# One Trainium2 core, gated cross-attention with experts: the weighted sums of a slot moved behind the next slot's first pair of scores

## The chip, the cores and the metric

The kernel runs on one core of one Trainium2 chip. The metric is the device time of one execution in microseconds (us); the median of the runs stands for a kernel. The engines are named as in the profile: PE (TensorE, matmul), PEld (its weight loads), DVE (VectorE), ACT (ScalarE), POOL (GpSimd), SP (SyncE, which issues DMAs).

## What is computed

Cut to what matters here:

```python
def layer(x, ctx):                       # x (16, 512, 256), ctx (16, 1601, 128), all f32
    n = layernorm(x)
    y = attention(n Wq, n Wk, n Wv, causal)          # 16 heads of 16
    y = y + attention(n Wcq, ctx Wck, ctx Wcv)       # 16 heads, 1601 keys
    x = x + tanh(g_xattn) * (y Wp + bp)
    n = layernorm(x)
    return x + tanh(g_ffn) * (top4_of_32_experts(n) + shared_expert(n))
```

For each head the softmax runs over the 512 causal keys of the text, and a second one over the 1601 keys of the context; the two weighted sums of values are added.

## The kernel before

**Three stages.** A short prologue (part "P") prepares batch 0. Then 16 parts follow, one for each batch ("F", 14 times "M", "L"), which do the attention. They also finish the batch before (output projection, second layer norm, router, shared expert, scatter to the experts' slots) and prepare the next one. A last part "X", the experts and a merge come after them. The change lies in the 16 parts alone.

**Slots.** A part is 68 slots. A slot is one tile of 128 keys against 512 queries for 4 heads: `slot_of(n)` gives for each group g of 4 heads (4 groups) 13 tiles of context keys ("cross", the last with 65 keys) and then 4 tiles of text keys ("self"). A self tile `kt` takes only the queries from 128*kt on. Counted through a part, the self slots are 13 to 16, 30 to 33, 47 to 50 and 64 to 67.

**What a slot holds.** PE writes scores transposed, keys on partitions, in pairs of heads: `scores(part, n, 0)` and `scores(part, n, 1)`, two matmuls each (L442), into a ring of three PSUM buffers, so that score i waits until exponential i-3 is done (L440). ACT takes the exponential of each (L627) into `prob`, which has two halves by the parity of the slot; it waits for the weighted sums of two slots ago. In self slots POOL zeroes the masked triangle of all four heads in one instruction (L966), after the fourth exponential, in `mask`, which stands in POOL's second half of the slot. PE then forms the weighted sums (`weighted`, L464): four f32 matmuls in four groups of 32 columns, shown as eight instructions, into one PSUM bank `outs` in which a softmax's 13 or 4 slots accumulate. For a cross slot `weighted(part, n)` waits until the fourth exponential of slot n is done, for a self slot until its mask is. At the first tile of a softmax it also waits for `copied`: ACT has copied the sums of the softmax before out of the bank (`outs`, L637), which stands at the end of ACT's slot, behind the four exponentials.

**Items.** The softmax's maxima are computed apart and a group ahead: PE writes tiles of scores with queries on partitions (L520, L527, L536 and L537) to a ring of four PSUM banks (`ring`), and DVE reduces each with a maximum (L780). These tiles and all the projections of the neighbouring batches are "items". `plan(kind)` writes the order out: it deals fixed items to half slots and fills the rest with maxima so that a load in estimated us is level. Each of the 136 half slots of a part has a list, `items[2 * n + pair]`, that every engine walks in the same order. What the change calls the maxima of a slot is such a list. Of the 52 cross slots of an "M" part, 23 have a list for their second half with at most two maxima of 512 columns and no projection in it. One of them is slot 39, where the router's softmax stands: `soft_a` on ACT waits for DVE. In slot 16 POOL comes to `inverse_root` (16 small instructions, L953 to L959, for the second layer norm), which waits for DVE's statistics and stands ahead of that slot's mask.

**The order on PE.** Engines take their instructions in the program's order. PE's order in a part is `run` of `pe_program`. ACT's is `exps`, items, `exps`, items, `outs` of the slot before; POOL's has the mask in the second half. The change touches `run` of `pe_program` alone.

Of the kernel before, what the change touches and what calls it, by code (L numbers as in the profile page):

```python
# [106 lines left out]
def slot_of(n):  # L107

    ch, r = divmod(n, SLOTS // 2)
    v, r = divmod(r, NCT + NQ)  # L110
    return (ch, v, "cross", r) if r < NCT else (ch, v, "self", r - NCT)


def shape_of(kind, kt):

    if kind == "cross":
        return (128 if kt < NCT - 1 else REST), 0, kt, T + 128 * kt
    return 128, 128 * kt, NCT + kt, 128 * kt
# [19 lines left out]
def value_items(ch):  # L138
    return [("value", ch, 4 * i, min(4, NCT - 4 * i)) for i in range(4)] + [("value", ch, NCT, NQ)]
# [92 lines left out]
def build_attention(nc, B, x, ctx_t, w, scr, stacks, wall):  # L232
# [6 lines left out]
    with ExitStack() as ctx:  # L239
# [151 lines left out]
        def read(eng, part, it, i=0, **how):  # L391

            p = PLANS[part.kind]
            eng.wait_ge(freed[p.bank[it, i]], part, p.turn[it, i], **how)
# [27 lines left out]
        def pe_program(eng):  # L422
# [8 lines left out]
            def scores(part, n, pair):  # L431
                ch, v, kind, kt = slot_of(n)
                m, q0, _, k0 = shape_of(kind, kt)
                qc = 0 if kind == "cross" else T
                g = 2 * ch + v
                for p in range(2):
                    j, i = 2 * pair + p, 4 * n + 2 * pair + p
                    k = i % SB
                    before = i - SB if i >= SB else max(j for j in range(4 * SLOTS) if j % SB == k) - 4 * SLOTS
                    pe.wait_ge(exped, part, before + 1)  # L440
                    pe.wait_ge(rowed[g], part, row_no(g))
                    eng.matmul(ps[0:m, k, q0:T], kst[g][0:KR + 2, j, k0:k0 + m],  # L442
                               qst[g][0:KR + 2, j, qc + q0:qc + T], start=True, stop=True).then_inc(scored.sem, 1)

            def weighted(part, n):

                ch, v, kind, kt = slot_of(n % SLOTS)
                m, q0, vi, _ = shape_of(kind, kt)
                last = kt == (NCT if kind == "cross" else NQ) - 1
                if kind == "cross":  # L450
                    pe.wait_ge(exped, part, 4 * n + 4)
                else:
                    pe.wait_ge(masked, part, 4 * (2 * ch + v) + kt + 1 - (16 if n < 0 else 0))
                if kt == 0:
                    pe.wait_ge(copied, part, 4 * ch + 2 * v + (kind == "self"))
                if n == 0:
                    for k in range(RB):
                        pe.wait_ge(freed[k], part, 0)
                if n == SLOTS // 2:
                    for it in value_items(1):  # L460
                        read(pe, part, it)
                for j in range(4):
                    hl = 4 * v + j
                    mm = eng.matmul(po[32 * j:32 * j + 32, q0:T], vt[ch][0:m, VW * vi + VE * hl:VW * vi + VE * hl + 32],  # L464
                                    prob[0:m, n % 2, j, q0:T], start=kt == 0, stop=last)
                    if j == 3:
                        mm.then_inc(summed.sem, 1)
# [120 lines left out]
            def run(part):  # L588
                items = PLANS[part.kind].items
                if part.kind in "PX":  # L590
                    for here in items:
                        for it in here:
                            item(part, it)
                    return
                for n in range(SLOTS):
                    for pair in range(2):
                        scores(part, n, pair)
                        for it in items[2 * n + pair]:
                            item(part, it)
                    if n or not part.first:  # L600
                        weighted(part, n - 1)

            start = Part("P", 0, B - 2)
            pe.wait_ge(loaded, start, LOADS)
            pe.wait_ge(consts, start, CONSTS)
            pe.wait_ge(setup, start, 3)
            run(start)
            run(Part("F", 0, B - 2))
            for b in range(1, B - 1):
                run(Part("M", b, B - 2))  # L610
# [1071 lines left out]
```

## Time and profile before

| what | us |
|---|---|
| median of 3 runs | 4988.99 (4988.46 to 4994.27) |
| profiled execution, its own time | 5012.8 |
| its span in the trace | 5011.0 |
| PE busy in the span | 4348.2 (87%) |
| DVE busy | 3558.0 (71%) |
| ACT busy | 2689.2 (54%) |
| POOL busy | 1685.3 (34%) |
| granted clock of PE, mean over the span | 0.957 |

The profiled execution took 5012.8 us, of which 1.8 lie outside the span; it is 0.5% longer than the median. Busy is the time in which an engine has an instruction at work. Matmuls are pipelined, and a row of two matmuls of 512 columns shows 0.60 us although the next matmul starts 0.44 after the first of them. So distances between starts are read here, not lengths, where the pace of PE matters.

### The profile page before, as it was taken

The page shows a single profiled execution, that of the slowest core. Times are in us where ns is not written, and L with a number is a line of the kernel's source. Part 1 is how long each engine was busy: PE and PEld are TensorE (multiplying, and loading weights), DVE is VectorE, ACT ScalarE, POOL GpSimd, SP SyncE. Part 2 cuts the span into 40 slices and gives each one's busy share as a digit, 9 for nine tenths or more (in the row PEclk, how much of TensorE's full clock was granted, in tenths as well). Part 3 has the DMA queues.
Part 4 walks back from the last instruction along what each step waited for, and adds up shares of the span by engine and source line. Part 5 has one row for each costly group of instructions (what it writes and reads, how often), then busy time and mean ns, then how long its engine had stood idle before and what let it go on. Part 6 is the DMA issues. An engine that isn't in the chain of part 4 may idle for free. (4 is left out here: it accounts for less than half of the span.)

```text
span 5011.0 us, 75640 instructions
## 1 busy us (share of the span) xinstructions
PE 4348.2 (87%) x25312; PEld 1888.4 (38%) x25312; DVE 3558.0 (71%) x7731; ACT 2689.2 (54%) x5523; POOL 1685.3 (34%) x2170
## 2 busy tenths in 40 slices
PE   4899999999999999999999999999999961777872
PEld 1333333333333333333333333334343411566662
DVE  4788878877778777878787878787878732344443
ACT  0565656565656565656565656565656550444441
POOL 3122323232323232323232323232323131577773
PEclk7999999999999999999999999999999985899996
DMA  4444545453544443445454544444544436788888
GB/s 91 81 89 78 108 78 108 79 107 80 102 84 102 82 104 82 105 78 109 77 108 77 109 77 108 78 108 78 105 81 101 69 95 153 130 137 134 136 138 251
DMA packets 363510, 513.36 MB, mean 102 GB/s; under 512 B 64052, under 2 KB 227766, under 8 KB 363190
## 3 DMA queue, kind: packets, MB, share of 16 engines
q1 hardware_dynamic: 252022, 372.60, 35.9%
q0 software_dynamic: 88064, 115.69, 13.3%
q10 hardware_dynamic: 23104, 20.97, 1.4%
q8 instruction: 181, 2.97, 0.3%
q14 instruction: 139, 1.14, 0.1%
HBM read 288.77 MB, written 201.29 MB: 98 GB/s over the span
## 5 line engine op out<-in xcount | busy, mean ns | idle before, releaser
L627 ACT ACTIVATE prob<-scores 128x512 f32<-128x512 f32 (+3 forms) x4352 | 2151.5, 560 | 1333.9 <-PE scores L442 1308.6
L780 DVE TENSOR_REDUCE pmx<-ring 128x1 f32<-128x512 f32 (+1 forms) x3328 | 2000.4, 662 | 188.9 <-PE ring L520 172.0
L442 PE MATMUL scores<-stacks 98*128 98x512 bf16 (+3 forms) x4352 | 1270.7, 369 | 71.1 <-ACT prob L627 36.5
L464 PE MATMUL outs<-prob,vt 128*32 128x512 f32 x8704 | 1099.9, 578 | 11.0 <-POOL prob L966 10.0
L520 PE MATMUL ring<-stacks 96*128 96x512 bf16 x3072 | 985.8, 389 | 90.5 <-DVE pmx L780 79.7
L442 PEld LDWEIGHTS scores<-stacks 98*128 98x128 bf16 (+1 forms) x4352 | 337.7, 99 | 1247.0 <-ACT prob L627 716.4
L1523 POOL DMA_INDIRECT scratch_sums<-e_yo,e_tok x320 | 497.9, 1556 | 230.8 <-DVE e_yo L1486 130.5
L780 DVE TENSOR_REDUCE mc<-ring 128x1 f32<-128x128 f32 (+3 forms) x1024 | 437.4, 482 | 151.2 <-PE ring L537 113.7
L966 POOL TENSOR_SCALAR_AFFINE_SELECT prob<-prob 128x512 f32<-128x512 f32 x256 | 168.5, 658 | 1075.0 <-ACT prob L627 1073.3
L520 PEld LDWEIGHTS ring<-stacks 96*128 96x128 bf16 x3072 | 303.0, 99 | 516.4 <-DVE pmx L780 244.4
L1035 POOL TENSOR_TENSOR split<-rest,split 128x512 bf16<-128x512 f32 (+1 forms) x224 | 218.8, 977 | 819.0 <-DVE split L858 818.5
L1345 PE MATMUL e_ph<-e_xt,e_we 128*128 128x256 f32 x1280 | 322.2, 395 | 129.8 <-ACT e_xt L1381 126.7
L855 DVE SCALAR_TENSOR_TENSOR rest<-ring,bcol,split 128x512 f32<-128x512 f32 (+1 forms) x224 | 153.1, 684 | 270.8 <-ACT split L661 268.8
L536 PE MATMUL ring<-stacks 96*128 96x128 bf16 (+3 forms) x1024 | 272.3, 309 | 55.9 <-DVE mc L780 20.1
L1345 PEld LDWEIGHTS e_ph<-e_xt,e_we 128*128 128x128 f32 x1280 | 232.1, 191 | 214.7 <-ACT e_xt L1381 171.5
L464 PEld LDWEIGHTS outs<-prob,vt 128*32 128x32 f32 x8704 | 172.4, 109 | 354.1 <-issue 316.0
L1486 DVE TENSOR_SCALAR e_yo<-e_py,e_wcol 128x256 f32<-128x256 f32 x320 | 140.1, 479 | 213.5 <-DMA scratch_sums<-e_yo,e_tok 195.3
L1024 POOL DMA_INDIRECT scratch_slots<-split,rows x256 | 253.4, 990 | 106.5 <-issue 69.8
L1390 ACT COPY e_we<-stacks 128x768 f32 x160 | 133.6, 835 | 155.5 <-issue 140.3
L661 ACT ACTIVATE split<-ring,bcol 128x512 bf16<-128x512 f32 (+1 forms) x224 | 142.2, 637 | 137.2 <-PE ring L491 107.9
L537 PE MATMUL ring<-maskb,identb 128*128 128x128 bf16 x1024 | 211.7, 223 | 0.0
L1466 DVE SCALAR_TENSOR_TENSOR e_sl<-e_th,e_ph 128x256 f32<-128x256 f32 x160 | 67.4, 421 | 189.9 <-ACT e_th L1400 189.9
(155 smaller groups left out, 3891.9 us busy)
## 6 DMA issues: line engine op xcount, KB each, us to landing
stacks<-scratch_parts SPq DMA_DIRECT2D x768, 128.0 KB, 7.1
stacks<-scratch_parts SPq DMA_DIRECT2D x384, 136.1 KB, 10.2
scratch_parts<-split SPq DMA_DIRECT2D x64, 768.0 KB, 4.4
e_xin<-scratch_slots SPq DMA_DIRECT2D x160, 289.0 KB
scratch_parts<-split SPq DMA_DIRECT2D x32, 816.8 KB, 4.5
num<-oc POOLq DMA_DIRECT2D x256, 64.0 KB
den<-scratch_inverses POOLq DMA_DIRECT2D x64, 256.0 KB, 9.0
ct<-in_ctx_t_dram SPq DMA_DIRECT2D x16, 800.5 KB, 8.1
```

The source lines that it names most:

```text
L442: eng.matmul(ps[0:m, k, q0:T], kst[g][0:KR + 2, j, k0:k0 + m], qst[g][0:KR + 2, j, qc + q0:qc + T], start=True, stop=True).then_inc(scored ...
L464: mm = eng.matmul(po[32 * j:32 * j + 32, q0:T], vt[ch][0:m, VW * vi + VE * hl:VW * vi + VE * hl + 32], prob[0:m, n % 2, j, q0:T], start=kt ...
L520: eng.matmul(dst, qst[g][0:KR, j, 128 * qt:128 * qt + 128], kst[g][0:KR, j, T + 512 * of:T + 512 * of + 512], start=True, stop=True).then_ ...
L536: eng.matmul(dst[:, 0:n], qst[g][0:KR, j, T + 128 * qt:T + n], kst[g][0:KR, j, 0:n], start=True, stop=False)
L537: eng.matmul(dst[:, 128 * qt:n], identb[:, :], maskb[:, :], start=False, stop=True).then_inc(ring.sem, 1)
L627: eng.activation(prob[0:m, n % 2, j, q0:T], ps[0:m, i % SB, q0:T], ACT.Exp, scale=SCALE).then_inc(exped.sem, 1)
L780: eng.tensor_reduce(dst, src, AX.X, ALU.max).then_inc(free_of(part, it), 1)
L966: eng.affine_select(out=prob[:, n % 2, :, q0:q0 + 128], in_=prob[:, n % 2, :, q0:q0 + 128], compare_op=ALU.is_ge, fill=0.0, base=0, patter ...
L1024: eng.indirect_dma_start(scr["slots"], bass.IndirectOffsetOnAxis(ap=rows[:, NQ * k + q:NQ * k + q + 1].bitcast(U32), axis=0), xs[:, ROW * ...
L1035: eng.tensor_tensor(last, rest[:, no % 2, 0:n], mid, ALU.subtract).then_inc(low.sem, 1)
L1345: op = eng.matmul(phd[i][:, m, :], we[u][:, c0:c0 + H], xt[i][:, kc, :], start=kc == 0, stop=kc == KC - 1)
L1523: eng.indirect_dma_start(scr[f"sums{i}"], bass.IndirectOffsetOnAxis(ap=tok[u][:, q:q + 1].bitcast(U32), axis=0), yo[i][:, q, :], None, com ...
```

## The change

In a slot n, PE's program had: scores of pair 0, first list of items, scores of pair 1, second list of items, weighted sums of slot n-1. With the change it has: scores of pair 0, weighted sums of slot n-1, first list, scores of pair 1, second list. No instruction is added or taken away; the other engines' programs and all waits' values are the same.

```diff
                 for n in range(SLOTS):
                     for pair in range(2):
                         scores(part, n, pair)
+                        if pair == 0 and (n or not part.first):
+                            weighted(part, n - 1)
                         for it in items[2 * n + pair]:
                             item(part, it)
-                    if n or not part.first:
-                        weighted(part, n - 1)
```

## Rows read from the trace of the kernel before

**Rows 1.** Page, busy time and slices: PE, DVE and PE's granted clock.

```profile
PE 4348.2 (87%) x25312; PEld 1888.4 (38%) x25312; DVE 3558.0 (71%) x7731; ACT 2689.2 (54%) x5523; POOL 1685.3 (34%) x2170
...
PE   4899999999999999999999999999999961777872
```

**Rows 2.** Busy time by stretch, a batch's worth: PE, PEld, DVE, ACT, POOL, clock, DMA, GB/s.

```profile
1770.00:2040.00 270.00, 251.57 (x1483) 94.22 (x1480) 216.35 (x469) 158.62 (x321) 75.90 (x116) 0.97 0.47 98
```

**Rows 3.** The scores' line: number, shortest/median/longest ns, first and last start.

```profile
L442 PE MATMUL scores<-stacks x4352: 217/379/634, 127.7 to 4102.5; 98*128 98x512 bf16 x151, 98*128 98x128 bf16 x12, 98*128 98x256 bf16 x12, 98*128 98x384 bf16 x12
```

**Rows 4.** Waits over the whole span: us in total, times, longest.

```profile
PE ring L520 <- DVE pmx L780: 79.7, 116, 5.4
...
PE scores L442 <- ACT prob L627: 36.5, 82, 1.2
```

**Rows 5.** Groups by line, engine PE: weighted sums and causal maxima, idle before them.

```profile
L464 PE MATMUL outs<-prob,vt 128*32 128x512 f32 x8704 | 1099.9, 578 | 11.0 <-POOL prob L966 10.0
...
L536 PE MATMUL ring<-stacks 96*128 96x128 bf16 (+3 forms) x1024 | 272.3, 309 | 55.9 <-DVE mc L780 20.1 <-DMA stacks<-scratch_parts 14.6 <-DVE rest L855 5.5
```

**Rows 6.** Timeline of PE, one light cross slot (slot 9 of a batch).

```profile
1900.32 0.60 PE L442 MATMUL scores<-stacks 98*128 98x512 bf16 x2
1900.75 0.60 PE L520 MATMUL ring<-stacks 96*128 96x512 bf16 x2
1901.28 1.06 PE L464 MATMUL outs<-prob,vt 128*32 128x512 f32 x8
1902.28 0.61 PE L442 MATMUL scores<-stacks 98*128 98x512 bf16 x2
```

**Rows 7.** Timeline of ACT in the same slot.

```profile
1899.65 2.18 ACT L627 ACTIVATE prob<-scores 128x512 f32<-128x512 f32 x4 [0.90 <-PE scores L442]
```

**Rows 8.** Timeline of DVE, slots 5 to 10 of that batch.

```profile
1887.58 18.05 DVE L780 TENSOR_REDUCE pmx<-ring 128x1 f32<-128x512 f32 x30 [0.87 <-PE ring L520]
```

**Rows 9.** Timeline of PE, the old sums in self slot 48.

```profile
2055.20 1.06 PE L464 MATMUL outs<-prob,vt 128*32 128x512 f32 x8
```

**Rows 10.** Timeline of POOL, the mask of slot 48.

```profile
2055.59 0.63 POOL L966 TENSOR_SCALAR_AFFINE_SELECT prob<-prob 128x512 f32<-128x512 f32 x1 [2.22 <-ACT prob L627]
```

**Rows 11.** Timeline of PE, slots 64 to 67 (end of the batch).

```profile
2112.33 1.06 PE L464 MATMUL outs<-prob,vt 65*32 65x512 f32 x8
...
2115.05 1.06 PE L464 MATMUL outs<-prob,vt 128*32 128x512 f32 x8
...
2120.03 0.59 PE L442 MATMUL scores<-stacks 98*128 98x512 bf16 x2 [0.51 <-DMA stacks<-mr]
```

**Rows 12.** Timeline of POOL, the masks of slots 64, 65 and 66.

```profile
2112.93 0.64 POOL L966 TENSOR_SCALAR_AFFINE_SELECT prob<-prob 128x512 f32<-128x512 f32 x1 [0.35 <-ACT prob L627]
2116.24 0.91 POOL L966 TENSOR_SCALAR_AFFINE_SELECT prob<-prob 128x512 f32<-128x512 f32 x1 [2.68 <-ACT prob L627]
2117.12 1.08 POOL L1035 TENSOR_TENSOR split<-rest,split 128x512 bf16<-128x512 f32 x1
2118.17 0.67 POOL L966 TENSOR_SCALAR_AFFINE_SELECT prob<-prob 128x512 f32<-128x512 f32 x1
```

**Rows 13.** Timeline of PE, slot 16 into 17.

```profile
1925.94 0.23 PE L536 MATMUL ring<-stacks 96*128 96x128 bf16 x1 [1.23 <-DVE mc L780]
...
1927.27 1.08 PE L464 MATMUL outs<-prob,vt 128*32 128x256 f32 x8
1928.28 1.03 PE L442 MATMUL scores<-stacks 98*128 98x512 bf16 x2
```

**Rows 14.** Timeline of POOL, the mask of slot 16, behind the Newton steps.

```profile
1930.14 0.64 POOL L966 TENSOR_SCALAR_AFFINE_SELECT prob<-prob 128x512 f32<-128x512 f32 x1
```

**Rows 15.** Timeline of PE, slots 39 and 41: where it waits for ACT and DVE.

```profile
2021.41 0.39 PE L442 MATMUL scores<-stacks 98*128 98x512 bf16 x1 [1.12 <-ACT prob L627]
...
2028.94 0.52 PE L520 MATMUL ring<-stacks 96*128 96x512 bf16 x1 [3.24 <-DVE pmx L780]
```

**Rows 16.** Busy time by stretch around slot 16 (columns as in the first such view).

```profile
1926.00:1930.00 4.00, 3.83 (x19) 1.19 (x20) 2.38 (x7) 1.07 (x2) 2.79 (x15) 0.58 0.00 0
```

## The prediction
> **What bounds the kernel now.** I read the page's slices first. PE is busy nine tenths or more in the 29 slices after the first two and before the fall at the end, 87% over the span [rows 1]. That is the stage of the 16 parts, the only one that the change touches. The 4352 score matmuls of that stage start between 127.7 and 4102.5 us [rows 3]: 3975 us for 1088 slots, 3.65 us a slot and 248 us a batch. In a stretch of 270 us PE is busy 251.6, DVE 216.4, ACT 158.6 and POOL 75.9 [rows 2]. So PE stands still for 18.4 us in 270, some 17 us a batch, and the rest is work in a fixed order. Then the waits: PE's largest kinds are small, 79.7 us for DVE to empty a bank and 36.5 us for ACT [rows 4], and in front of the 8704 rows of weighted sums it is idle for only 11.0 us in all [rows 5]. That last number is what the change puts at stake. The sums find their operands ready today because they come nearly a whole slot after the exponentials that they need.
>
> **What moves.** Nothing is added or removed. Seen along the queue, the end of a slot was: second list of items of slot n, weighted sums of n-1, first scores of n+1. It becomes: second list of n, first scores of n+1, weighted sums of n. Two things change: the scores come 1.0 us earlier against the items (the sums' pitch, 1901.28 to 1902.28 [rows 6]), and each set of sums comes one slot earlier. The pitches themselves I cost at nothing: each of score, sum and tile still has a neighbour of another kind, and only their order differs. No DMA is issued by PE, and no queue of POOL, SP, ACT or DVE has a step moved past another.
>
> **The new wait, and who is behind it.** The sums of n now wait for the fourth exponential of n (self slots: for the mask after it), with only the second list and one pair of scores as cover. Queued behind them on PE are the first list of n+1, which DVE needs, and the second pair of scores, which ACT needs. I price it by one subtraction: the time at which the operands are ready, less the time at which PE would come to the sums. The latter is today's start of the sums of n-1 plus the pitch of a pair of scores.
>
> *Light cross slots.* In slot 9 the old sums start at 1901.28, so the new place is 1901.28 + 0.44 = 1901.72 [rows 6]. The fourth exponential ends at 1899.65 + 2.18 = 1901.83 [rows 7], and about 0.06 us (my estimate, from the scale of the rows' distances) passes on the way: a wait of 0.16 us. With a third tile of 0.22 in the second list it is gone. The lists have 23 cross slots with at most two such tiles in the second half, one of them slot 39. Where ACT has another pass in front of the exponentials it is 0.3 to 0.5. I take 0.27 x 22 = 6.0 us a batch. At a softmax's first tile the copy of the bank comes on top; self slots hide it beside the mask, and the few others are within this figure.
>
> *Self slots.* In slot 48 the new place is 2055.20 + 0.22 (a pair of 256 columns, half of 0.44) = 2055.42, the mask ends at 2055.59 + 0.63 = 2056.22 [rows 9, 10]: 0.8 us. Of the eleven self slots before the last group, slot 16 left out, three have a projection or a long list behind them and cost nothing. For the other eight I let the pitch of the list and POOL's own work vary around this one, 0.1 to 1.3 us, and take 0.66 as their mean: 5.3 us a batch.
>
> *End of the batch.* Slot 64: place 2112.33 + 0.33 (the 0.44 for 384 columns), mask ready 2113.57: 0.9. Slot 65: place 2115.05 + 0.22, mask ready 2117.15: 1.9. Slot 66 the same way gives 1.5, but there POOL's 1.08 us of other work came just before the mask and would run under the stall ahead: 0.9. Slot 67 is covered by the wait for a DMA (0.51) that PE has anyway [rows 11, 12]. Sum 3.7.
>
> *Slot 16.* POOL's Newton steps, which wait for DVE, stand ahead of the mask, and it ends at 1930.14 + 0.64 = 1930.78 [rows 14]. The new place is 1927.27 + 0.44 = 1927.71 [rows 13]: 3.1 us.
>
> *Slot 39.* ACT is held by the router's softmax. PE's scores already wait for it, 1.12 us [rows 15]; the sums add one exponential or two: 1.4 us.
>
> The five together: 6.0 + 5.3 + 3.7 + 3.1 + 1.4 = 19.5 us a batch, gross.
>
> **What is given back.** Where PE stands for DVE a little later, the new wait only takes that one's place. Slot 39 is followed by 3.24 us for DVE in slot 41 [rows 15]: all 1.4 are absorbed. In slots 5 to 10 DVE runs 30 maxima in 18.05 us without a gap [rows 8]; 0.60 for each and five or six tiles a slot is what PE supplies, so DVE has a full ring, and half of the light slots' loss (3.0) is taken by waits for banks that vanish. For self slots I take half as well (2.6), for the waits in front of the causal maxima [rows 5]; for slot 16, 1.1; for the end of the batch 0.7, from the 0.51 there [rows 11] and part of PE's short waits for ACT [rows 4]. Sum 8.8. A gain beside it: a second pair of scores no longer follows closely on the first, so part of the 36.5 us (2.3 a batch) for ACT goes away [rows 4]; I take 1.3, with nothing and 2.3 as ends. Against it stands the clock. After a wait of 1.23 us in slot 16 the granted clock is 0.58 over 4 us, a part of them at 1.2 instead of 2.4 GHz, and a pair of scores takes 1.03 instead of 0.60 [rows 13, 16]. The new waits of 1 to 3 us lie in such places; one more such fall costs up to 4 x 0.42 = 1.7 us a batch. I take 0.9, between nothing and that.
>
> **The sum.** 19.5 - 8.8 - 1.3 + 0.9 = 10.3 us a batch, 165 us for 16. The profiled execution would go from 5012.8 to 5178. The runs' median lies 24 us under the profiled time; with the same difference kept it goes from 4989 to 5154.
>
> **A rule against this reading.** The rows say that PE's order binds, since it is busy 251.6 of 270 us. The Trainium skill (Perfetto Trace Analysis, Identifying the Most-Contended Engine) holds that matmul busy time does not tell how near PE is to its limit, that the share of LDWEIGHTS and the flops do, and that the engine with the highest occupancy is the one to work on. By that rule PE has room (PEld is 94.2 of 270), DVE with 216.4 is the engine to look at, and a wait on PE would cost nothing: the first rival. No row shown contradicts the rule for PE's arithmetic; but the rows' starts follow each other without a gap, and an order that leaves no gap loses what a wait adds.
>
> **Rivals.**
> 1. *Absorbed.* DVE is the bound, PE's stalls replace its waits for banks. For it: the unbroken 18.05 us of DVE [rows 8]. Against it: DVE is free a fifth of the stage [rows 2], and self slots cluster where lists are short. In full: 19.5 less the 17 us or so that PE now stands a batch leaves 0 to 3 us, 4989 to 5037. Chance 0.12; in about half of it the difference is under 0.2%.
> 2. *Faster.* ACT is the hidden bound: it stands 0.90 us before the exponentials of slot 9, waiting for scores [rows 7]. With scores 1.0 us earlier, ACT's exponentials start earlier against DVE's tiles, and PE's waits for ACT and the small ones in front of scores go. It decides if the waits for masks are mostly under today's idle time. All 36.5 us and the 11.0 in front of the sums [rows 4, 5] would give 4989 - 48 = 4941. Chance 0.07.
> 3. *Nothing absorbed.* DVE and ACT start later by as much as PE does, so their later waits stay what they were: 19.5 x 16 = 312, 5301. Chance 0.13.
>
> My forecast, part absorbed, has 0.68.
>
> **Range.** The low end lies inside rival 1: 5015, at 1.6 us a batch. The high end is just under rival 3's 5301: 5295. Below lie rival 2 (0.07) and the lower half of rival 1 (0.06), above some 0.06 of rival 3: 0.19 outside. A measurement of this kernel tells 0.2%, 10 us, from no change. Faster by more than that: rival 2, 0.07. Within it: the lower half of rival 1, 0.06. Slower: the rest, 0.87.
>
> **What would show it.** In the profile after: idle time in front of the weighted sums of 100 to 250 us in place of 11.0, mostly released by POOL's mask and ACT's exponentials; less than 79.7 us in front of the maxima for DVE and less than 36.5 for ACT; in a batch, a stall of 2 to 3 us at slot 17's sums and of 1 to 2 at slots 65 to 67; light slots of 3.1 to 3.2 us instead of the 3.0 that DVE's five tiles take; the mean granted clock a little lower; everything after 4103 us shifted and not longer. It would be wrong if the sums waited as foreseen and the slots' total stayed (rival 1), or if POOL's mask came well under 0.3 us after PE reaches the sums.

## The result and the profile after

The changed kernel takes 5229.88 us (median of 4 runs, 5225.95 to 5240.8) against 4989.59 for the kernel before: ratio 1.0483, 95% interval 1.0465 to 1.0501. It is 240 us slower. The forecast was 5154, with a range of 5015 to 5295.

The page of the changed kernel, busy times and slices; they answer to [rows 1]:

```profile
span 5224.2 us, 75703 instructions
...
PE 4432.8 (85%) x25312; PEld 1908.7 (37%) x25312; DVE 3573.2 (68%) x7731; ACT 2673.8 (51%) x5523; POOL 1680.7 (32%) x2170
...
PE   4899898989898999898989899989999982488883
```

PE has the same 25312 matmuls, yet it is busy 85 us longer, and slices of 8 stand among the nines. The score matmuls start between 127.6 and 4327.0 us, where [rows 3] had 127.7 to 4102.5. So the stage of the 16 parts grew by 225 us, 14.0 a batch, and nothing else did: what stands behind the last score took 11 us less. (The profiled execution of the kernel before lies 23 us above its median, that of the changed kernel 4 us below, so the two spans differ by 213 us where the medians differ by 240.) Now the groups of PE, in the order that the page gives them (idle time in front of each, and what ended it); they answer to [rows 5] and to the waits of [rows 4]:

```profile
L442 PE MATMUL scores<-stacks 98*128 98x512 bf16 (+3 forms) x4352 | 1301.1, 373 | 63.2 <-ACT prob L627 49.1 <-issue 6.3
L464 PE MATMUL outs<-prob,vt 128*32 128x512 f32 x8704 | 1109.7, 583 | 209.9 <-POOL prob L966 151.6 <-ACT oc L637 24.0 <-issue 0.8
L520 PE MATMUL ring<-stacks 96*128 96x512 bf16 x3072 | 990.3, 394 | 53.5 <-DVE pmx L780 47.1 <-issue 0.9 <-DMA stacks<-scratch_parts 0.3
L536 PE MATMUL ring<-stacks 96*128 96x128 bf16 (+3 forms) x1024 | 282.8, 324 | 49.0 <-DVE mc L780 22.7 <-DMA stacks<-scratch_parts 14.5 <-DVE rest L855 5.4
```

In front of the weighted sums (L464) PE now idles 209.9 us in place of 11.0, nearly three quarters of it for POOL's mask. In front of the maxima (L520) the wait for DVE fell from 79.7 to 47.1. The rest is in the first numbers: the same scores are busy 1301.1 us where they were 1270.7. The mean granted clock of the two profiled executions is 0.943 after and 0.957 before. The traces' records of the clock have two levels, 2.4 GHz and half of that, so a mean of 0.957 over 5011 us is 0.043 x 2 x 5011 = 431 us at the lower one, and 0.943 over 5224 us is 596 us. All of the growth lies in the stage of the 16 parts: by the records it has 143 us at the lower level before, in 32 spells, and 301 us after, in 46. PE is busy for 135 us of the first and 254 us of the second.

In a stretch of 270 us as in [rows 2] every engine is busy for less time, since less of the work fits in:

```profile
1770.00:2040.00 270.00, 245.27 (x1449) 93.57 (x1450) 204.90 (x435) 151.68 (x310) 74.17 (x119) 0.97 0.44 87
```

**The dearest place: slot 17.** The timeline of PE in one batch, where the sums of slot 16 now stand (they were in [rows 13]):

```profile
2029.08 0.23 PE L536 MATMUL ring<-stacks 96*128 96x128 bf16 x1 [1.44 <-DVE mc L780]
...
2030.11 0.60 PE L442 MATMUL scores<-stacks 98*128 98x512 bf16 x2
2033.94 0.65 PE L464 MATMUL outs<-prob,vt 128*32 128x128 f32 x8 [3.23 <-POOL prob L966]
...
2035.45 1.06 PE L442 MATMUL scores<-stacks 98*128 98x512 bf16 x2
...
2037.59 1.06 PE L442 MATMUL scores<-stacks 98*128 98x512 bf16 x2
```

POOL's timeline there, the last Newton step and the mask behind it:

```profile
2033.10 0.20 POOL L959 TENSOR_TENSOR rstd<-rstd,newt 128x4 f32<-128x4 f32 x1
2033.25 0.63 POOL L966 TENSOR_SCALAR_AFFINE_SELECT prob<-prob 128x512 f32<-128x512 f32 x1
```

And the busy times of two stretches of 4 us (PE, PEld, DVE, ACT, POOL, clock):

```profile
2032.00:2036.00 4.00, 2.06 (x13) 0.86 (x14) 0.73 (x2) 0.00 (x0) 1.55 (x6) 0.55 0.00 0
2036.00:2040.00 4.00, 4.00 (x16) 0.96 (x15) 2.45 (x4) 2.65 (x5) 2.02 (x4) 0.59 0.15 17
```

The sums wait 3.23 us for the mask. ACT does nothing in the first stretch and DVE 0.73 us, because the tiles and the scores that they need stand behind the sums in PE's queue. The granted clock is 0.55 and then 0.59; before it was 0.58 in one such stretch [rows 16]. Two pairs of scores take 1.06 us instead of 0.60.

**The end of the batch**, timeline of PE (compare [rows 11]):

```profile
2225.04 1.06 PE L464 MATMUL outs<-prob,vt 128*32 128x512 f32 x8 [0.78 <-POOL prob L966]
...
2229.68 0.86 PE L464 MATMUL outs<-prob,vt 128*32 128x384 f32 x8 [1.07 <-POOL prob L966]
...
2232.32 1.08 PE L464 MATMUL outs<-prob,vt 128*32 128x256 f32 x8 [0.69 <-POOL prob L966]
...
2234.00 1.03 PE L442 MATMUL scores<-stacks 98*128 98x512 bf16 x2 [0.26 <-ACT prob L627]
```

Three waits for masks in a row, then the next batch's first scores at the lower clock. The 256 columns of 2232.32 take 1.08 us where [rows 11] has 1.06 for 512. At the higher clock the same sums take 0.64, as in the kernel before:

```profile
2118.89 0.64 PE L464 MATMUL outs<-prob,vt 128*32 128x256 f32 x8
```

**A light cross slot**, PE's timeline in slots 9 and 10:

```profile
2000.32 0.60 PE L442 MATMUL scores<-stacks 98*128 98x512 bf16 x2
2000.88 1.06 PE L464 MATMUL outs<-prob,vt 128*32 128x512 f32 x8
...
2003.42 0.59 PE L442 MATMUL scores<-stacks 98*128 98x512 bf16 x2
2004.10 1.06 PE L464 MATMUL outs<-prob,vt 128*32 128x512 f32 x8
```

In slot 9 (2000.32 to 2003.42) stand the sums of slot 8. They start 0.56 us after the scores, hardly more than the pair's pitch of 0.44 and the 0.09 that [rows 6] show in front of sums (1901.28, less 1900.75 and two tiles of 0.22). Slot 9 is 3.10 us long here; over the batches its mean is 0.03 us above that of the kernel before. The sums of slot 9, which the forecast priced, stand in slot 10. They start 0.68 us after the scores, 0.15 more than 0.44 and 0.09, and slot 10 is 0.16 us longer in the mean. Such a wait is shorter than the tail that the profile shows of the scores ahead, so it hardly shows as idle time.

The starts of the 4352 score matmuls give the length of every slot. The mean over the 14 middle parts, as the difference to the kernel before in us a batch, summed by place, for the changed kernel and for the experiments below (the first column is the kernel before, run again):

```
slots                 again  after  newton  nomask  nomask  cross  self   half   half   half
                                    after   after   before  early  early  later  newton cross
17 to 20               0.0    4.4   -0.3    -0.1     0.1    0.2    4.4    2.0   -0.6   -1.4
64 to 67, 0 and 1      0.1    5.3    5.9     2.0     0.0    0.9    4.9    0.3    0.4    0.4
13-16, 30-35, 47-51   -0.1    2.9    2.7     0.6     5.3    2.0    1.9   -0.3    0.8   -0.2
39 to 46              -0.4    0.1    0.8     0.5     0.0    0.1    0.2    0.8    0.6    0.5
all others            -0.2    1.2    0.0     0.0    -0.7   -0.2    0.2   -3.1   -1.4   -1.1
sum                   -0.5   13.7    9.1     3.0     4.6    3.1   11.6   -0.4   -0.2   -1.8
```

Four columns (newton after, nomask after, cross early, half later) come from a chip that gave no profile of the kernel before and on which that kernel is faster (4955 us) than where it was profiled (5012.8). So their sums are too low: by the ratios below these runs lose 4.1 to 4.3 us a batch more than the table says (half later 3.7 and not -0.4). In the other columns the ratio and the sum agree within 1.3 us. Where the 4 us stand can't be read from these traces, and it is not known either whether the kernel before is fast on that chip for a reason that any edit of the order undoes.

### The profile page after: what moved, and what is told of

The parts are those of the page before. It is cut to its first block and busy times, and to the rows that moved or that the text cites. A ratio compares the mean times of both kernels' runs of the same rounds, so it can differ in the third digit from the quotient of the medians.

```text
span 5224.2 us, 75703 instructions
## 1 busy us (share of the span) xinstructions
PE 4432.8 (85%) x25312; PEld 1908.7 (37%) x25312; DVE 3573.2 (68%) x7731; ACT 2673.8 (51%) x5523; POOL 1680.7 (32%) x2170
## 5 line engine op out<-in xcount | busy, mean ns | idle before, releaser
L627 ACT ACTIVATE prob<-scores 128x512 f32<-128x512 f32 (+3 forms) x4352 | 2157.0, 560 | 1491.8 <-PE scores L442 1436.0
L442 PE MATMUL scores<-stacks 98*128 98x512 bf16 (+3 forms) x4352 | 1301.1, 373 | 63.2 <-ACT prob L627 49.1
L464 PE MATMUL outs<-prob,vt 128*32 128x512 f32 x8704 | 1109.7, 583 | 209.9 <-POOL prob L966 151.6
L520 PE MATMUL ring<-stacks 96*128 96x512 bf16 x3072 | 990.3, 394 | 53.5 <-DVE pmx L780 47.1
L442 PEld LDWEIGHTS scores<-stacks 98*128 98x128 bf16 (+1 forms) x4352 | 423.1, 101 | 621.5 <-ACT prob L627 221.3
L520 PEld LDWEIGHTS ring<-stacks 96*128 96x128 bf16 x3072 | 264.8, 99 | 922.5 <-issue 566.6
L464 PEld LDWEIGHTS outs<-prob,vt 128*32 128x32 f32 x8704 | 175.6, 110 | 609.8 <-ACT prob L627 231.6
L536 PE MATMUL ring<-stacks 96*128 96x128 bf16 (+3 forms) x1024 | 282.8, 324 | 49.0 <-DVE mc L780 22.7
L1024 POOL DMA_INDIRECT scratch_slots<-split,rows x256 | 252.7, 987 | 105.7 <-issue 69.7
L536 PEld LDWEIGHTS ring<-stacks 96*128 96x128 bf16 x1024 | 102.4, 102 | 260.1 <-issue 170.9
```

Source lines behind the costliest of these rows:

```text
L520: eng.matmul(dst, qst[g][0:KR, j, 128 * qt:128 * qt + 128], kst[g][0:KR, j, T + 512 * of:T + 512 * of + 512], start=True, stop=True).then_ ...
L536: eng.matmul(dst[:, 0:n], qst[g][0:KR, j, T + 128 * qt:T + n], kst[g][0:KR, j, 0:n], start=True, stop=False)
L627: eng.activation(prob[0:m, n % 2, j, q0:T], ps[0:m, i % SB, q0:T], ACT.Exp, scale=SCALE).then_inc(exped.sem, 1)
L1024: eng.indirect_dma_start(scr["slots"], bass.IndirectOffsetOnAxis(ap=rows[:, NQ * k + q:NQ * k + q + 1].bitcast(U32), axis=0), xs[:, ROW * ...
```

## Experiments

Theory W is the prediction's: the sums wait for operands that come too late, masks above all. The rival O says that the order itself costs, by the 1.0 us of sums that now separates scores from items. Ratios are always against the kernel before on the same chip. That kernel came out at 4955, 5005 and 4992 us on the chips of the three groups, so times are not compared between groups. On the first (4955) ran the sums half a slot later, the cross sums alone, the Newton steps and the masks left out of the changed kernel; on the second (5005) the kernel before again, the self sums alone, and the Newton steps and the masks on the kernel before; on the third (4992) the rest. Single slots of the table between 39 and 56, where the chips differ most, are only good to about 1 us.

**The kernel before again.**

> The kernel before, unchanged, for a profile from the same chip as the experiments: ratio 1.00. What it tells: which slots are longer in the experiments than in this execution, rather than in the one shown first, whose chip gives times 0.7% longer. Both theories expect 4950 to 4960 us. If slots 40 to 44 and 55 differ from the first profile, the differences that I read there belong to the chip and not to the order.

Ratio 1.0001 (0.9991 to 1.0012), 5005 us. It was meant for the chip of the first group and ran on another, so that chip's own profile of the kernel before is missing. Outside slots 39 to 56 and 16 to 20 its slots repeat the first profile to 0.01 us nearly everywhere. So what the table shows in slots 64 to 20 is hardly an effect of the chip, as far as these two profiles tell.

**The changed kernel again.**

> The changed kernel again, on the chip of this group, so that the group's other runs are compared with it and not across chips (the kernel before has come out at 4955, 4989 and 5005 us on different ones). Both theories expect the ratio 1.048 to the kernel before.

Ratio 1.0485 (1.0468 to 1.0502). The loss repeats, on the chip of the third group; which chip gave the first result isn't on record.

**The sums half a slot later.**

```diff
                         scores(part, n, pair)
-                        if pair == 0 and (n or not part.first):
+                        if pair == 1 and (n or not part.first):
                             weighted(part, n - 1)
```

> The weighted sums of slot n-1 stand behind the second pair of scores of slot n, half a slot later than in the changed kernel and one list of items earlier than before. Theory W (the loss is waiting for operands that come too late: exponentials, and masks above all): the cover grows by a whole list and a pair of scores, some 1.1 us, more than nearly all waits but slot 16's; I expect 5000 to 5060 us. Theory O (the loss is in the order itself: the 1.0 us of sums that stands between the first scores and the first list, and so holds up ACT or DVE): the sums still stand between a pair of scores and a list, so most of the loss stays, 5170 to 5230.

Ratio 1.0123 (1.0106 to 1.0139), 5014.58 us, inside W's range. The weighted sums still stand between a pair of scores and a list, and three quarters of the loss is gone: O falls. Idle time in front of the sums in this run:

```profile
L464 PE MATMUL outs<-prob,vt 128*32 128x512 f32 x8704 | 1103.7, 580 | 30.1 <-POOL prob L966 29.0
```

By the ratio 60 us are left. Slots 17 to 20 hold 32 of them (2.0 us a batch), as W has it for the mask behind the Newton steps; where the other 28 stand is not shown.

**The Newton steps behind the mask**, on the changed kernel, in POOL's program:

```diff
                         if pair == 1:
                             mask(part, n)
+                        late = [it for it in left if pair == 0 and it == ("outproj", NQ - 1)]
                         for it in left:
-                            second(part, it)
-                        left = items[2 * n + pair]
-                        for it in left:
+                            if it not in late:
+                                second(part, it)
+                        left = late + items[2 * n + pair]
+                        for it in items[2 * n + pair]:
                             item(part, it)
```

> The changed kernel, with POOL's Newton steps of the second norm put behind the mask of slot 16 instead of ahead of it. Theory W: slots 17 and 18, which are 4.8 us a batch longer in the changed kernel, lose their cause; 4 to 5 us a batch, so 5230 - 70 = 5150 to 5165 us, and the wait of the sums for the mask falls by about 50 us. Theory O: no difference, 5230.

Ratio 1.0439 (1.0421 to 1.0456), 5169.59 us, 5 us above W's 5150 to 5165. By the table slots 17 to 20 lose all of their 4.4 us a batch, 70 us in 16. The sums' row:

```profile
L464 PE MATMUL outs<-prob,vt 128*32 128x512 f32 x8704 | 1113.5, 585 | 166.2 <-POOL prob L966 105.7 <-ACT oc L637 27.8
```

The wait for the mask fell from 151.6 to 105.7, by 46 us. The ratio fell by 0.0044 only, 22 us, while the time itself lies 60 us under the changed kernel's. It ran on the chip on which the kernel before takes 4955 us, and the changed kernel was not run there, so the size of the gain stays open between these two. The place and the mechanism don't.

**The same edit on the kernel before.**

> The kernel before with POOL's Newton steps of the second norm behind the mask of slot 16. There the sums come a slot later and don't wait for that mask, so theory W expects no change beyond 10 us (4945 to 4965). If it is slower or faster by more, the Newton steps' own place matters for the norm that waits for them, and the run on the changed kernel has to be read with that taken off.

Ratio 0.9992 (0.9982 to 1.0001). The Newton steps' place matters only where a set of sums stands close behind.

**Both edits together.** The sums half a slot later, and the Newton steps behind the mask:

> The sums half a slot later than in the changed kernel, and POOL's Newton steps behind the mask of slot 16. The run with the first edit alone gave ratio 1.0123, and nearly all of its loss stood in slots 17 and 18 (3.3 us a batch, 52 us), where PE waits for the mask behind the Newton steps. Theory W: that goes, ratio 1.000 to 1.003. Theory O: the sums stand between scores and a list as before, 1.012.

Ratio 1.0019 (1.0008 to 1.0030), 12 runs: 52 us less than the first edit alone by the ratios, of which the table has 42 in slots 17 to 20. The idle time in front of the sums is gone:

```profile
L464 PE MATMUL outs<-prob,vt 128*32 128x512 f32 x8704 | 1099.4, 578 | 3.3 <-POOL prob L966 2.2
```

This is W's number. The order with sums between scores and a list costs next to nothing, 5 us, when no operand is late; the changed kernel costs 4.8% on this same chip.

**Masks left out**, on the changed kernel (the call of `mask` is gone, so the text attention is not causal, and self slots wait like cross slots):

```diff
-                if kind == "cross":
-                    pe.wait_ge(exped, part, 4 * n + 4)
-                else:
-                    pe.wait_ge(masked, part, 4 * (2 * ch + v) + kt + 1 - (16 if n < 0 else 0))
+                pe.wait_ge(exped, part, 4 * n + 4)
```

> The changed kernel without the masks of the self slots (POOL's 256 instructions are left out, so text attention is not causal); the sums of self slots wait for the fourth exponential as cross slots do. Theory W: all that hangs on the mask goes, about 10 of the 13.7 us a batch, 5050 to 5090 us. Theory O: about 5230, since POOL is 32% busy and no bound.

Ratio 1.0241 (1.0223 to 1.0259), 5069.38 us, within W's 5050 to 5090. The stage is 10.7 us a batch shorter than the changed kernel's by the table and 7.5 by the ratios. Both compare two chips, so the size stays open between them: three quarters of the loss by the table, half of it by the ratios. The row of the sums in this run (its line numbers are three lower):

```profile
L461 PE MATMUL outs<-prob,vt 128*32 128x512 f32 x8704 | 1098.0, 577 | 103.9 <-ACT oc L634 69.1 <-ACT prob L624 0.5
```

A second gate shows that the mask had covered: ACT's copy of the finished sums out of the bank, 69.1 us where the changed kernel has 24.0.

**Masks left out of the kernel before.**

> The kernel before without the masks of the self slots (left out as in the run on the changed kernel). The sums hardly wait for a mask there (10 us), so theory W expects 4940 to 4960. A theory by which POOL's work or its use of the memory slows the others expects the same gain here as in the changed kernel, about 2.4%, 4840.

Ratio 1.0121 (1.0104 to 1.0138): slower without the masks. Neither W (no change) nor the theory by which POOL's work slows the others (2.4% faster) has this, and the last run's control is not clean. The loss has one place, slot 49, 6.0 us a batch longer; in the run without masks on the changed kernel that slot is 0.15 us longer. ACT's and DVE's timelines in slot 49:

```profile
2090.80 1.25 ACT L624 ACTIVATE prob<-scores 128x256 f32<-128x256 f32 x4 [3.43 <-remote]
```

```profile
2090.85 2.81 DVE L777 TENSOR_REDUCE mc<-ring 128x1 f32<-128x512 f32 x7 [3.17 <-remote]
```

POOL issues five scatters there, 1.27 us apart, with no mask between them, and then both engines stand for more than 3 us for something that the profile does not name. What it is stays open, and whether the scatters have to do with it too. It does not touch the slots on which the argument rests: the rows of the table for 17 to 20 and 64 to 1 are at zero in this run.

**Only the sums of cross slots moved, and only those of self slots.** This is the edit of the first run, on the kernel before; that of the second has "self" in both places:

```diff
                         scores(part, n, pair)
+                        if pair == 0 and (n or not part.first) and slot_of((n - 1) % SLOTS)[2] == "cross":
+                            weighted(part, n - 1)
 ...
-                    if n or not part.first:
+                    if (n or not part.first) and not (slot_of((n - 1) % SLOTS)[2] == "cross"):
                         weighted(part, n - 1)
```

> Only the sums of cross slots take the new place, those of self slots stay at the slot's end. Theory W: cross slots wait for exponentials alone; the changed kernel's cross slots away from the self slots came out nearly unchanged, so some 2 to 3 us a batch, 5020 to 5050 us. Theory O: three quarters of the sums (52 of 68 in a part) are in the new place, so three quarters of the 240 us: about 5170.

Ratio 1.0239 (1.0222 to 1.0256), 5072.72 us: a miss for both, above W's 5020 to 5050 and below O's 5170.

> The other half of the change: only the sums of self slots take the new place, those of cross slots stay at the slot's end. Theory W, with the cross slots' run at 2.4%: the rest of 4.8%, 2.0 to 2.8%, 5055 to 5095 us, and the sums wait for the mask about as long as in the changed kernel (some 150 us). Theory O: 16 of 68 sums are in the new place, a quarter of the 240 us: 5010 us.

Ratio 1.0352 (1.0335 to 1.0369), 5182.55 us: far above O's quarter (5010), and above W's 2.0 to 2.8% as well. The row of the sums:

```profile
L464 PE MATMUL outs<-prob,vt 128*32 128x512 f32 x8704 | 1111.5, 584 | 134.4 <-POOL prob L968 110.2 <-ACT oc L639 21.9 <-issue 0.7
```

The halves add up to 5.9% where the whole is 4.8%. One reason may be the chip: the cross half is from the one whose ratios lie 4 us a batch, 1.4%, above the table. Another can be read. With cross sums alone moved, slots 30 and 31 have no sums between the second list of the one and the first list of the other, PE fills the ring sooner, and slot 31 is 2.0 us longer, where the changed kernel's is 0.5. The row of the causal maxima names a releaser that it doesn't name in either kernel, DVE's maxima of whole tiles (this kernel's line numbers are two higher):

```profile
L536 PE MATMUL ring<-stacks 96*128 96x128 bf16 (+3 forms) x1024 | 271.7, 309 | 66.0 <-DVE pmx L782 20.9 <-DVE mc L782 19.6 <-DMA stacks<-scratch_parts 14.1
```

By the table the 16 self sums a batch carry 11.6 of 13.7 us and the 52 cross sums 3.1. By the ratios it is 3.5% and 2.4%. The exact share of the cross slots stays open; that self slots carry most, though they are a quarter of the sums, does not.

**The copy taken earlier**, on the changed kernel, in ACT's program:

```diff
                         exps(part, n, pair)
+                        if pair == 0 and (n or not part.first):
+                            outs(part, n - 1)
                         for it in items[2 * n + pair]:
                             item(part, it)
-                    if n or not part.first:
-                        outs(part, n - 1)
```

> The changed kernel with ACT's copy of a softmax's sums moved from the slot's end to behind the first pair of exponentials, where its sums are now done already. Theory W: the wait of the sums for the copy (24.0 us in the changed kernel) goes, 10 to 25 us less than the changed kernel, ratio 1.043 to 1.046; if ACT, now behind the late sums of slot 16, holds up the second pair of exponentials there, part of that is lost. Theory O: 1.048.

Ratio 1.0446 (1.0427 to 1.0464) against 1.0485 for the changed kernel in the same group, 14 us less. The wait for the copy is gone from the row:

```profile
L464 PE MATMUL outs<-prob,vt 128*32 128x512 f32 x8704 | 1114.8, 586 | 184.9 <-POOL prob L966 150.7 <-issue 0.3
```

Against the changed kernel on the same chip, slots 35 and 52 are 1.0 and 0.5 us shorter, 24 us in 16 batches, and slots 39 to 46 together 1.2 us longer. 24 us of wait bought 14 us of time; in front of the maxima the wait for DVE rose again, from 48.0 to 67.6 us between the two profiles of that group. So some of a wait taken away comes back as another: that is absorption, seen in a number.

**A version that beats both.** Cross sums behind the second pair of scores of the next slot, self sums at the slot's end:

```diff
+                        if pair == 1 and (n or not part.first) and slot_of((n - 1) % SLOTS)[2] == "cross":
+                            weighted(part, n - 1)
 ...
-                    if n or not part.first:
+                    if (n or not part.first) and not (slot_of((n - 1) % SLOTS)[2] == "cross"):
                         weighted(part, n - 1)
```

> The sums of cross slots behind the second pair of scores of the next slot, those of self slots at the slot's end as before; no sum comes nearer to a mask. Theory W: cross sums have a list and a pair of scores more of cover than in the changed kernel, so no wait; the gains of slots 24, 55 and 56 (3 us a batch in the run with all sums half later) may stay: ratio 0.990 to 1.003. Theory O: 1.01.

Ratio 0.9978 (0.9966 to 0.9991) over 11 runs, 4977.1 against 4992.3 us, inside W's range. It is a small gain, just clear of its noise. The idle time in front of the sums is that of the kernel before:

```profile
L464 PE MATMUL outs<-prob,vt 128*32 128x512 f32 x8704 | 1096.9, 576 | 10.2 <-POOL prob L968 10.1
```

The gain stands in slots with a long first list (slot 24 is 1.1 us shorter, slot 47 0.9); part of it is paid back in slots 14 and 44.

## Why the prediction was right, and where its sizes were off

**Side and mechanism.** Slower, by waits of the sums for masks and exponentials: shown by the idle time of 209.9 us in front of them and by four runs that take a gate or its lateness away (half a slot later, Newton steps, masks, copy), each of which takes time off, and most of all by the run with both edits, which leaves 3.3 us of that idle time and a loss of 0.2%. The idle time was forecast at 100 to 250 us. Rival 1 (absorbed) is false as a whole: in the stage PE's other visible waits fell by some 59 us, 37 of them in front of the maxima, against 198 new ones. Rival 2 (faster) is false: ACT stands for scores 1436.0 us where it stood 1308.6. Rival 3 (nothing absorbed), at 5301, is too high, but 5230 lies about as near to it as to the forecast of 5154: far less was absorbed than I took.

**The rule of the Trainium skill** (Perfetto Trace Analysis, Identifying the Most-Contended Engine) would have taken PE for an engine with room. The runs decide for the rows here: PE's LDWEIGHTS share stayed at 37 to 38%, and delaying its queue cost 4.8%. An engine can have room by that measure and still set the time by its order.

**The sum.** 165 us forecast, 240 measured, 225 in the two profiles' stage. The 225 can be split by PE's time: 198 us of new idle time in front of the sums, 59 less in front of everything else, and 85 us more busy, that is 12.4 - 3.7 + 5.3 = 14.0 a batch. My terms were 19.5 of waits, 8.8 + 1.3 given back and 0.9 for the clock. So the waits and what they give back were both taken too large, and that these two errors nearly cancel is luck. By terms, in us a batch:

- *Clock:* taken 0.9 for the whole. This is the term that failed most in the net sum. PE is busy for 119 us more at the lower level than before. If work takes about twice as long there (the rows have 1.06 for 0.60 and, for sums of 256 columns, 1.08 for 0.64), half of that is lost: 59 us, 3.7 a batch, an estimate. The other 26 us of busy time are probably waits that the profile does not show as idle, as in slot 10; that is not shown.
- *Light cross slots:* taken 6.0 - 3.0 = 3.0, measured 1.2 in all slots away from self slots. The price of slot 9 was right (0.16 forecast, 0.15 in the rows), and so was the number: the sums start late in this way in 22 places a batch. What failed is the mean of 0.27. All 22 lie between 0.13 and 0.18, 3.5 us in sum; the 0.3 to 0.5 that I took where ACT has another pass in front do not appear. The 3.0 that a full ring was to give back fail too: in slots 4 to 10, where DVE ran without a gap [rows 8], the waits sum to 0.5 us and the slots are longer by just that. Gains elsewhere, in slots 55 and 56 above all, where chips differ, bring the sum to 1.2.
- *Slot 16 and 17:* taken 3.1 - 1.1 = 2.0, measured 4.4 in slots 17 to 20. The wait itself was right (3.23 against 3.1). What failed is that 1.1 would be absorbed, and the clock beside it: DVE stood idle in the wait instead of catching up, and the following 4 us ran at 0.59.
- *End of the batch:* taken 3.7 - 0.7 = 3.0, measured 5.3 in slots 64 to 1. The waits sum to 0.78 + 1.07 + 0.69 = 2.5 us where I had 3.7. They cost more than they last. One reason is shown, the clock that has fallen at their end; that ACT's and POOL's next results come later, since their scores stand behind the sums, is argued from the order.
- *Other self slots:* taken 2.7, measured 2.9. *Slot 39:* taken 0, measured 0.1 in slots 39 to 46, where single slots move by up to 2.5 either way.
- *Gain:* 1.3 was taken for shorter waits for ACT; by the row of the scores those rose from 36.5 to 49.1, against the sign that I had named.
- *The copy:* its wait was put inside the light slots' figure; the row of the sums has 24.0 us for it, 1.5 a batch.

A small slip of reading: PE's row of slices has 30 nines before the fall, not 29. Nothing rests on it.

## What to carry to other kernels

In a queue that takes its instructions in order, moving a consumer nearer to its producer saved nothing here, where only ACT's copy waited for the sums (70.0 us in all before, 1.5 after) and nothing waited for the copy on PE; what matters is how late each of its gates can come, and the latest one (a mask behind other work on a slow engine) sets the price. Before moving it, subtract place from readiness at every kind of slot, count what stands behind it for the other engines, and add what the clock costs behind stalls of one to three microseconds (here some 3.7 us a batch of 14, by the estimate above). Don't count on waits elsewhere to absorb it before a row shows them in the same slots. Read each subtraction with the order as it will be, since the move also shifts the producer.

## What the runs showed of the hardware that was not expected

**VectorE held by GpSimd.** In slot 41 the kernel before has two small products on DVE that take 1.90 and 1.31 us; the same two take 0.29 each a few microseconds later. DVE's and POOL's timelines:

```profile
2025.05 1.90 DVE L820 TENSOR_TENSOR split<-down,split 128x128 f32<-128x128 f32 x1
2026.98 1.31 DVE L821 SCALAR_TENSOR_TENSOR split<-split 128x128 f32<-128x128 f32 x1
...
2031.49 0.29 DVE L820 TENSOR_TENSOR split<-down,split 128x128 f32<-128x128 f32 x1
2031.82 0.29 DVE L821 SCALAR_TENSOR_TENSOR split<-split 128x128 f32<-128x128 f32 x1
```

```profile
2024.46 2.34 POOL L1000 TENSOR_TENSOR num<-num,den 128x1024 f32<-128x1024 f32 x1 [8.65 <-DMA den<-scratch_inverses]
2026.88 1.26 POOL L1004 TENSOR_TENSOR yg<-num 128x512 f32<-128x512 f32 x1
```

Each of the two long DVE instructions ends 0.15 us after the POOL instruction beside it. Of the 64 instances of the first product, 13 overlap one of these POOL instructions. Twelve of them start behind POOL's and take 1.84 to 2.41 us; the thirteenth starts 0.07 us ahead of it and takes 0.29, as all others do. The Trainium skill (SBUF — State Buffer, Who interferes with whom) says that a DVE instruction with two SBUF inputs and GpSimd's reads hold a shared port in turns, for a whole instruction. The rows agree, with 2.34 us for the holder and 1.90 for the one that waits. Slots 40 to 44 are also among those in which chips differ; whether this is the reason was not tried.

**A stall that the profile does not name.** Without the masks the kernel before stands for more than 3 us in slot 49 on ACT and DVE together, behind a close run of POOL's scatters. The cause is open.

**Chips differ.** The kernel before took 4955, 4992 and 5005 us on three of them, up to 1.0%, with runs of each agreeing within 0.4%. Between the first of them and the others even the effect of an edit may differ by some 4 us a batch, 1.4%; that is not shown, since one profile is missing.
